# Moving four element-wise steps of a recurrent stage to GpSimd, one square to VectorE, and dropping three matmul uses

## The chip, the cores and the metric

One core of a Trainium2 chip runs the whole program. The metric is device time in microseconds (us) of one execution. TensorE (PE in the rows) does matmuls, VectorE (DVE), ScalarE (ACT) and GpSimd (POOL) do element-wise work, SyncE (SP) issues transfers. Each engine works through its own list of instructions in order and waits on semaphores that other engines raise.

## The reference, cut to what matters

The model has 12 sub-layers; each is followed by a layer norm over the 128 features, so that what enters a stage has mean zero over the features. The changed one is the seventh, a stack of four recurrent layers (RWKV) on 8192 tokens (128 sequences of 64 tokens), 128 features:

```python
for l in range(4):
    h = layer_norm(x, ln1_w[l]); prev = time_shift(h)        # prev: the token before
    k, v = (mix of h and prev by tm_mix_k / tm_mix_v) @ tm_k_w / tm_v_w
    r = sigmoid((h * tm_mix_r + prev * (1 - tm_mix_r)) @ tm_r_w)
    x = x + (r * wkv_scan(k, v, decay, first)) @ tm_o_w
    h = layer_norm(x, ln2_w[l]); prev = time_shift(h)
    kk = (h * cm_mix_k + prev * (1 - cm_mix_k)) @ cm_k_w      # 128 -> 512
    vv = square(relu(kk)) @ cm_v_w                            # 512 -> 128
    rr = sigmoid((h * cm_mix_r + prev * (1 - cm_mix_r)) @ cm_r_w)
    x = x + rr * vv
return layer_norm(x, lnf_w)
```

`wkv_scan` is a recurrence over the tokens: a running maximum, a numerator and a denominator, both weighted by exponentials, and their quotient.

## The kernel before, in words

Function `rwkv` (L2121) is this stage. Features lie on the 128 partitions, tokens along the free side; all is float32. A tile is 512 tokens (8 sequences of 64), so a layer has 16 tiles and the stage 64 *turns* m = 0 to 63 (layer = m // 16). The residual stream `xw` stays in SBUF, centred over the features: matmuls with `center` (identity minus 1/128) keep it so.

A matmul of 512 columns is issued as two instructions on 128x512 float32; I count such a pair as one *call*. A turn has these steps, by engine:

- TensorE: `variance1` (1 call), `keys` (2: now and previous token), `values` (2), `receptance` (1, on an input mixed beforehand), `output` (1), `variance2` (1), `receptance2` (2: `rnow` on the token, `rold` on the token before, summed in PSUM), `hidden` in two halves (4), `contract` in two halves (4), `centred` (1). In the first 16 turns `enter` (L2192, 1 call) makes the centred copy of the input.
- ScalarE: `copy_entered` (first 16 turns), `square1`, `rstd1` (Ln, Exp), `half_mixed_r`, `exp_ab`, `exp_g`, `ln_denominator`, `exp_r`, `ln_r`, `reciprocal`, `square2`, `rstd2`, `half_mixed`, `rectified` and `squared` for each half of the hidden layer (1024 elements a partition each), `exp_rr`, `ln_rr`, `sigmoid_rr`.
- VectorE: `normal1` (L2484) writes hp1, `mix_r`, `running_max`, `exponents_ab` (two instructions), `exponent_g`, `clamp_g`, `clamp_r`, `weighted`, `scan_den`, `scan_num`, `bonus`, `numerator`, `denominator` (L2569), `denominator_r` (L2576), `quotient` (L2581), `residual1` (L2586), `normal2` (L2590) writes hp2, `mix_k`, `clamp_rr`, `gated`, `residual2`. Between turns of the first layer `prepare(l)` scales the weights of layer l.
- GpSimd has nothing to do in this stage. SyncE issues the loads of the weights, seven to a layer, and then the loads of the next stages.

The order on each engine is written out by `interleaved` (L168): each step has a place in us, turn m's copy of it stands at m * PERIOD + place (PERIOD 17.9), and all are sorted by that number. These numbers order the instructions of one engine and nothing else; the semaphores set the time. So about four turns are in flight at once: while TensorE does `variance1` of turn m, it does `keys` of m-1, `output` of m-2 and `hidden` of m-3. After the last layer 16 short end turns (`end_sum`, `end_close` and others) make the final norm; their first ones are interleaved with the last main turns.

```python
    order = sorted((start + (m - first) * period + place, g, j, m) for g, (first, turns, start, period, steps) in enumerate(groups)
                   for j, (place, _) in enumerate(steps) for m in range(first, first + turns))
```

Of the kernel before, what the change touches and what calls it, by code (L numbers as in the profile page):

```python
# [2120 lines left out]
def rwkv(nc, k, d, ahead=()):  # L2121
# [6 lines left out]
    with ExitStack() as ctx:  # L2128
# [62 lines left out]
        def _(pe):
            def enter(m):  # L2192
                if m:
                    pe.wait_ge(ln1, m)
# [99 lines left out]
            interleaved((0, NT, 0, PERIOD, ((0.0, enter),)),  # L2294
                        (0, TURNS, 0, PERIOD, (
                            (10.1, variance1), (20.6, keys), (25.6, values), (24.1, receptance), (44.6, output),
                            (52.6, variance2), (59.8, lambda m: hidden(m, 0)), (58.7, receptance2),
                            (63.5, lambda m: hidden(m, 1)), (70.3, lambda m: contract(m, 0)),
                            (70.8, lambda m: contract(m, 1)), (76.1, centred))),
                        (TURNS, NT, END, END_PERIOD, ((3.2, variance1), (16.2, end_sum), (21.2, end_variance2))))  # L2300

        @block.scalar
        def _(act):
# [125 lines left out]
            interleaved((0, NT, 0, PERIOD, ((4.2, copy_entered),)),  # L2429
                        (0, TURNS, 0, PERIOD, (  # L2430
                            (5.4, square1), (20.8, half_mixed_r), (16.8, rstd1), (28.1, exp_r), (36.8, ln_r),
                            (38.5, ln_denominator), (31.6, exp_ab), (30.3, exp_g), (41.1, reciprocal),
                            (50.5, square2), (53.2, rstd2), (57.8, half_mixed),
                            (62.7, lambda m: rectified(m, 0)), (63.4, lambda m: squared(m, 0)),
                            (67.5, lambda m: rectified(m, 1)), (69.9, lambda m: squared(m, 1)),
                            (61.6, exp_rr), (62.1, ln_rr), (63.9, sigmoid_rr))),
                        (TURNS, NT, END, END_PERIOD, ((0.0, square1), (6.8, rstd1), (17.5, end_square2), (24.4, end_rstd2))))

        @block.vector
        def _(dve):  # L2440
# [128 lines left out]
            def denominator(m):  # L2569
                dve.wait_ge(g_ready, m + 1)  # L2570
                dve.wait_ge(den_ready, m + 1)
                if m:
                    dve.wait_ge(ln_low, m)
                dve.tensor_tensor(flat(dn[:])[:, :, 1:S], ex[:, 0, :, 1:S], den[:, :, 0:S - 1], ALU.add).then_inc(low, 1)

            def denominator_r(m):  # L2576
                dve.wait_ge(ln_low, m + 1)
                dve.wait_ge(er_ready, m + 1)
                dve.tensor_tensor(tokens(dl[:]), er[:], tokens(dl[:]), ALU.add).then_inc(low_r, 1)

            def quotient(m):  # L2581
                dve.wait_ge(rec, m + 1)
                dve.wait_ge(top, m + 1)
                dve.tensor_tensor(gv[:], gv[:], tokens(dl[:]), ALU.mult).then_inc(wkv, 1)

            def residual1(m):  # L2586
                dve.wait_ge(o_mm, m + 1)
                dve.tensor_tensor(xw[:, at(m)[1]], xw[:, at(m)[1]], ps[:, 1, :], ALU.add).then_inc(xc2, 1)

            def normal2(m):  # L2590
                dve.wait_ge(rs2, m + 1)
                if m:
                    dve.wait_ge(rr_mm, m)
                dve.tensor_tensor(hp2[:, :, 1:S1], flat(xw[:, at(m)[1]]), flat(rsb[:]), ALU.mult).then_inc(h2, 1)
# [22 lines left out]
            def end_close(m):  # L2617
# [6 lines left out]
                            (21.3, normal1), (30.4, mix_r), (32.3, clamp_r), (31.0, running_max), (34.3, exponents_ab),  # L2624
                            (31.9, exponent_g), (32.7, clamp_g), (37.0, weighted), (37.7, scan_den), (38.2, scan_num),
                            (34.9, bonus), (40.0, numerator), (39.1, denominator), (42.8, denominator_r),
                            (49.4, quotient), (52.7, residual1), (60.2, normal2), (62.6, mix_k), (66.0, clamp_rr),
                            (75.9, gated), (80.3, residual2))),
                        (1, NL - 1, PERIOD, PERIOD, ((21.3, prepare),)),
                        (TURNS, NT, END, END_PERIOD, ((15.8, normal1), (33.6, end_close))))  # L2630


# [1338 lines left out]
```

## Time and profile before

| | us |
|---|---|
| median of 3 runs (4816.67 to 4822.48) | 4822.15 |
| the profiled execution | 4821.5 |
| its span, first to last instruction | 4819.6 |
| the stage `rwkv` in it, 1859.5 to 3001.8 | 1142.3 |
| TensorE busy in the stage | 1125.4 |
| VectorE busy in the stage | 995.6 |
| ScalarE busy in the stage | 961.9 |
| GpSimd busy in the stage | 0 |

The busy times are unions of the intervals of the instructions; two neighbouring instructions of an engine overlap a little, so that the distance between two starts (called a *slot* below) is shorter than the duration of the first. A row of a timeline has the start in us, the duration in us, engine, line, operation, output and inputs; in brackets the idle time before it and what ended it. "L_attn_ps" and "L_xattn_ps" are PSUM, all other tiles SBUF; "L_attn_er" stands for `er` and `er2`, "L_attn_hp" for `hp1` and `hp2`.

### The profile page before, as it was taken

The numbers are of one execution on the slowest core, as the hardware profiler recorded it, in microseconds if no ns is written. First come the engines' busy times: TensorE is split into PE (matmuls) and PEld (weight loads), VectorE is DVE, ScalarE is ACT, GpSimd is POOL, SyncE is SP. The second block draws the span as 40 slices with busy tenths as digits, with TensorE's granted clock in tenths as the row PEclk, the third lists the DMA queues.
The fourth block names the chain that finished last, engine by engine and source line by source line (L and its number), as shares of the span: only waits on it lengthen the run. The fifth ranks groups of instructions, "written<-read, shape, count | busy, mean of one in ns | idle before, by whom it ended". The sixth has DMA issues, their size and how long they took to land. (4 is left out here: it accounts for less than half of the span.)

```text
span 4819.6 us, 101682 instructions
## 1 busy us (share of the span) xinstructions
PE 4417.6 (92%) x37631; PEld 2907.1 (60%) x37631; DVE 3409.0 (71%) x5379; ACT 3123.7 (65%) x5579; POOL 1471.2 (31%) x1948
## 2 busy tenths in 40 slices
PE   8999788889969987999999999789979989999888
PEld 6767556557757764444444444467657767777665
DVE  7978777567763337889999995653349966666748
ACT  6878677567764336888888888653248844444356
POOL 3444354114407760000000000047734412222327
PEclk9999999889989999999999999899999999999999
DMA  3000000000021122000000000311130000000110
GB/s 106 3 2 3 2 1 1 1 13 3 3 63 51 52 69 84 1 1 1 1 1 1 1 1 20 110 31 53 53 104 3 3 2 1 1 2 1 57 55 36
DMA packets 124460, 119.57 MB, mean 25 GB/s; under 512 B 19536, under 2 KB 104528, under 8 KB 123216
## 3 DMA queue, kind: packets, MB, share of 16 engines
q1 hardware_dynamic: 106576, 77.38, 5.2%
q0 software_dynamic: 17408, 35.69, 2.6%
q8 instruction: 318, 5.21, 0.5%
q14 instruction: 158, 1.29, 0.1%
HBM read 82.60 MB, written 30.41 MB: 23 GB/s over the span
## 5 line engine op out<-in xcount | busy, mean ns | idle before, releaser
L2683 POOL TENSOR_TENSOR L_xattn_E<-L_xattn_E,L_xattn_rz 128x256 f32<-128x256 f32 x16 | 10.2, 635 | 1277.6 <-DVE L_xattn_rz L2839 1277.6
L1759 POOL DMA_INDIRECT L_ffn_xg<-L_ffn_xrows,L_ffn_take x272 | 263.2, 968 | 281.1 <-DVE L_ffn_take L2054 198.8
L1823 PEld LDWEIGHTS L_ffn_ps<-L_ffn_early_down,L_ffn_mT 128*128 128x128 f32 x1904 | 246.8, 191 | 105.8 <-issue 79.8
L1765 POOL DMA_INDIRECT L_ffn_yrows<-L_ffn_yo,L_ffn_put x272 | 268.3, 987 | 99.8 <-issue 59.8
L1803 PE MATMUL L_ffn_ps<-L_ffn_up,L_ffn_xT 128*128 x544 | 259.2, 559 | 19.6 <-issue 8.1
L2919 POOL TENSOR_TENSOR L_xattn_E<-L_xattn_E,L_xattn_rz 128x1024 f32<-128x1024 f32 x64 | 123.7, 1932 | 471.5 <-DVE L_xattn_rz L3139 471.5
L1823 PE MATMUL L_ffn_ps<-L_ffn_early_down,L_ffn_mT 128*128 x1904 | 259.0, 276 | 2.5 <-DVE L_ffn_yo L2084 1.3
L2263 PE MATMUL L_attn_ps<-L_attn_rl,L_attn_wcv 128*128 128x512 f32 x512 | 240.6, 592 | 0.0
L2247 PE MATMUL L_attn_ps<-L_attn_mix,L_attn_wck 128*128 128x512 f32 x512 | 240.6, 592 | 0.0
L1913 ACT ACTIVATE L_ffn_mT<-L_ffn_ps 128x512 f32<-128x512 f32 x136 | 81.2, 597 | 236.9 <-PE L_ffn_ps L1812 236.9
L2073 DVE TENSOR_TENSOR L_ffn_m<-L_ffn_b,L_ffn_ps 128x512 f32<-128x512 f32 x136 | 93.6, 688 | 188.4 <-PE L_ffn_ps L1803 188.4
L2069 DVE TENSOR_TENSOR L_ffn_m<-L_ffn_sg,L_ffn_ps 128x352 f32<-128x352 f32 x136 | 70.9, 521 | 212.3 <-ACT L_ffn_sg L1903 212.3
L988 DVE TENSOR_REDUCE L_xattn_mx<-L_xattn_ps 128x16 f32<-128x1024 f32 x128 | 156.1, 1219 | 69.0 <-PE L_xattn_ps L812 69.0
L334 POOL TENSOR_TENSOR L_attn_Kbd<-L_attn_Kt,main_head_of_row 128x1024 f32<-128x1024 f32 x64 | 121.1, 1893 | 258.0 <-issue 249.5
L750 POOL TENSOR_TENSOR L_xattn_Kbd<-L_xattn_Kt,main_head_of_row 128x1024 f32<-128x1024 f32 x64 | 121.1, 1892 | 238.8 <-issue 233.1
L565 DVE TENSOR_TENSOR L_attn_ps<-L_attn_ps,L_attn_bias 128x512 f32<-128x512 f32 x256 | 164.9, 690 | 20.6 <-PE L_attn_ps L398 20.5
L1095 POOL TENSOR_SCALAR L_ffn_aq<-L_ffn_aq,L_ffn_qinv 128x512 f32<-128x512 f32 x64 | 126.9, 1997 | 165.0 <-ACT L_ffn_aq L1245 165.0
L2263 PEld LDWEIGHTS L_attn_ps<-L_attn_rl,L_attn_wcv 128*128 128x128 f32 x512 | 97.4, 190 | 122.4 <-issue 122.4
L2247 PEld LDWEIGHTS L_attn_ps<-L_attn_mix,L_attn_wck 128*128 128x128 f32 x512 | 92.7, 190 | 127.0 <-issue 92.7
L586 DVE TENSOR_REDUCE L_attn_mx<-L_attn_ps 128x16 f32<-128x1024 f32 x128 | 156.3, 1221 | 3.3
L824 PE MATMUL L_xattn_ps<-main_ident,L_xattn_E 128*128 128x128 f32 x1024 | 145.6, 281 | 14.1 <-ACT L_xattn_Qt L875 10.2
L596 DVE TENSOR_TENSOR L_attn_E<-L_attn_ps,L_attn_mx 128x1024 f32<-128x1024 f32 x128 | 156.1, 1220 | 2.3
(616 smaller groups left out, 13175.0 us busy)
## 6 DMA issues: line engine op xcount, KB each, us to landing
L_ffn_row_hot<-L_ffn_yrows SPq DMA_DIRECT2D x32, 256.0 KB, 3.0
L_ffn_col_hot<-L_ffn_yrows SPq DMA_DIRECT2D x32, 256.0 KB, 3.4
L_ffn_w<-in_L_ffn_e_W SPq DMA_DIRECT2D x32, 256.0 KB, 4.3
L_ffn_xrows<-L_ffn_xtok SPq DMA_DIRECT2D x42, 192.0 KB, 2.1
L_ffn_xg<-L_ffn_xrows,L_ffn_take POOLq DMA_INDIRECT x272, 2.5
L_ffn_yrows<-L_ffn_yo,L_ffn_put POOLq DMA_INDIRECT x272, 2.3
main_x<-in_xT SPq DMA_DIRECT2D x8, 512.0 KB, 7.5
main_ctx<-in_ctxT SPq DMA_DIRECT2D x4, 1024.0 KB, 11.5
```

What stands on the lines that cost most here:

```text
L565: b = dve.tensor_tensor(scores if in_place else E[t % 2][:, 8 * at:8 * at + 8, :].rearrange("p (a h) k -> p a (h k)", a=2), scores, bias_s ...
L586: dve.tensor_reduce(mx[t % 2][:, 16 * half:16 * half + 16], score_rows(half, t), AX, ALU.max) \
L596: dve.tensor_tensor(E[u][:, rows, :], score_rows(half, t), mx[u][:, rows].rearrange("p (a o) -> p a o", o=1).to_broadcast([P, 16, S]), ALU ...
L824: m = pe.transpose(to[:, j * P:(j + 1) * P], E[t % 2][:, row:row + 2, :], k["ident"][:])
L988: dve.tensor_reduce(mx[t % 2][:, 16 * half:16 * half + 16], score_rows(half), AX, ALU.max) \
L1095: m = pool.tensor_scalar(aq[u][:, j, :], aq[u][:, j, :], ROUND, qinv[u][:, 1, j:j + 1], ALU.subtract, ALU.mult)
L1759: pool.indirect_dma_start(xg[t % RING][:], None, xrows, bass.IndirectOffsetOnAxis(ap=take[:, t:t + 1], axis=0)) \
L1765: pool.indirect_dma_start(yrows, bass.IndirectOffsetOnAxis(ap=put[:, t:t + 1], axis=0), yo[t % RING][:], None).then_inc(scattered[t % RING ...
L1803: g = pe.matmul(ps[u][:, 0, 0:F], xT[u][:], up[:, bass.ds(at, F)], start=True, stop=True)
L1823: g = pe.matmul(ps[1][:, 3, 0:P], mT[u][0:rows[a], a * P:(a + 1) * P], down[a][:, bass.ds(at, P)], start=(a == 0), stop=(a == FT - 1))
L2247: r = pe.matmul(ps[:, 5 + a % 2, :], wck[:, at(m)[0], a * P:(a + 1) * P], mix[:], start=True, stop=True)
L2263: r = pe.matmul(ps[:, 7, :], wcv[:, at(m)[0], a, :], rl[:, a, :], start=(a == 0), stop=(a == FT - 1))
```

## The change

Receptance2's input is mixed before the matmul: ScalarE's new `half_mixed_r2` and VectorE's new `mix_r2` make `rmix2`, and `receptance2` is one call on it; `rold`, its load and its scaling go. `denominator`, `denominator_r`, `quotient` and `normal2` go from VectorE's list to a list of GpSimd. The square of the second hidden half goes from ScalarE to VectorE, as a product of the tile with itself. `enter` and `copy_entered` go; the first layer reads `xres` in their place. All places are new; PERIOD and the end turns' period are not.

```diff
-                for tile, j in ((wo, 3), (rnow, 4), (rold, 4)):
+                for tile, j in ((wo, 3), (rnow, 4)):
...
-            def enter(m):
-                if m:
-                    pe.wait_ge(ln1, m)
-                pe.matmul(ps[:, 0, :], center[:], xres[:, m * CT:(m + 1) * CT], start=True, stop=True).then_inc(c_mm, 1)
...
             def receptance2(m):
-                pe.wait_ge(h2, m + 1)
+                pe.wait_ge(rmixed2, m + 1)
                 if m:
                     pe.wait_ge(z, m)
-                pe.matmul(ps[:, 7, :], rnow[:, l, :], hp2[:, :, 1:S1], start=True, stop=False)
-                pe.matmul(ps[:, 7, :], rold[:, l, :], hp2[:, :, 0:S], start=False, stop=True).then_inc(rr_mm, 1)
+                pe.matmul(ps[:, 7, :], rnow[:, l, :], rmix2[:], start=True, stop=True).then_inc(rr_mm, 1)
...
+            interleaved((0, TURNS, 0, PERIOD, (
+                            (6.8, variance1), (20.0, keys), (27.3, values), (32.9, receptance), (46.1, output),
+                            (52.9, variance2), (61.4, lambda m: hidden(m, 0)), (61.0, receptance2),
+                            (66.5, lambda m: hidden(m, 1)), (71.2, lambda m: contract(m, 0)),
+                            (72.1, lambda m: contract(m, 1)), (76.8, centred))),
...
-                act.activation(sqa[:], xw[:, at(m)[1]], ACT.Square).then_inc(sq1, 1)
+                act.activation(sqa[:], before(m), ACT.Square).then_inc(sq1, 1)
...
+            def half_mixed_r2(m):
+                l = at(m)[0]
+                act.wait_ge(h2, m + 1)
+                if m:
+                    act.wait_ge(rr_mm, m)
+                act.activation(flat(rmix2[:]), hp2[:, :, 1:S1], ACT.Identity, scale=cnow[:, l, 1:2]).then_inc(half_rmix2, 1)
...
+            interleaved((0, TURNS, 0, PERIOD, (
+                            (-9.1, square1), (13.3, half_mixed_r), (-0.9, rstd1), (28.8, exp_r), (30.9, ln_r),
+                            (28.3, ln_denominator), (19.4, exp_ab), (23.8, exp_g), (34.0, reciprocal),
+                            (38.7, square2), (45.3, rstd2), (48.7, half_mixed), (48.0, half_mixed_r2), (54.9, lambda m: rectified(m, 0)), (55.1, squared),
+                            (60.1, lambda m: rectified(m, 1)),
+                            (61.0, exp_rr), (64.2, ln_rr), (64.5, sigmoid_rr))),
...
+        @block.gpsimd
+        def _(pool):
+            def denominator(m):
+                pool.wait_ge(g_ready, m + 1)
+                pool.wait_ge(den_ready, m + 1)
+                if m:
+                    pool.wait_ge(ln_low, m)
+                pool.tensor_tensor(flat(dn[:])[:, :, 1:S], ex[:, 0, :, 1:S], den[:, :, 0:S - 1], ALU.add).then_inc(low, 1)
+
+            def denominator_r(m):
+                pool.wait_ge(ln_low, m + 1)
+                pool.wait_ge(er_ready, m + 1)
+                pool.tensor_tensor(tokens(dl[:]), er[:], tokens(dl[:]), ALU.add).then_inc(low_r, 1)
+
+            def quotient(m):
+                pool.wait_ge(rec, m + 1)
+                pool.wait_ge(top, m + 1)
+                pool.tensor_tensor(gv[:], gv[:], tokens(dl[:]), ALU.mult).then_inc(wkv, 1)
+
+            def normal2(m):
+                pool.wait_ge(rs2, m + 1)
+                if m:
+                    pool.wait_ge(mixed, m)
+                    pool.wait_ge(rmixed2, m)
+                pool.tensor_tensor(hp2[:, :, 1:S1], flat(xw[:, at(m)[1]]), flat(rsb[:]), ALU.mult).then_inc(h2, 1)
+
+            pool.wait_ge(w_steps, 1)
+            staggered(TURNS, PERIOD, (39.9, denominator), (48.8, denominator_r), (50.0, quotient), (58.1, normal2))
...
+            def mix_r2(m):
+                l = at(m)[0]
+                dve.wait_ge(half_rmix2, m + 1)
+                dve.scalar_tensor_tensor(flat(rmix2[:]), hp2[:, :, 0:S], cold[:, l, 1:2], flat(rmix2[:]), ALU.mult, ALU.add) \
+                    .then_inc(rmixed2, 1)
+
+            def squared(m):
+                dve.wait_ge(relu, 2 * m + 2)
+                dve.tensor_tensor(rl[:, 2:4, :], rl[:, 2:4, :], rl[:, 2:4, :], ALU.mult).then_inc(srb, 1)
...
+            interleaved((0, TURNS, 0, PERIOD, (
+                            (14.8, normal1), (22.4, mix_r), (32.4, clamp_r), (25.1, running_max), (25.5, exponents_ab),
+                            (25.7, exponent_g), (27.3, clamp_g), (32.5, weighted), (30.7, scan_den), (35.1, scan_num),
+                            (36.7, bonus), (40.6, numerator), (44.9, residual1), (55.1, mix_k), (54.7, mix_r2), (68.0, squared),
+                            (61.4, clamp_rr),
+                            (72.4, gated), (74.0, residual2))),
```

Sorted by these places, one stretch of the changed lists reads:

- VectorE: gated, bonus, mix_r2, mix_k, residual2, mix_r, numerator, running_max, exponents_ab (2), clamp_rr, exponent_g, residual1, clamp_g, scan_den, squared, clamp_r, weighted, normal1, scan_num.
- ScalarE: rectified (first half), squared (first half), exp_ab, square2, exp_g, rectified (second half), exp_rr, square1, rstd2 (2), ln_denominator, ln_rr, sigmoid_rr, exp_r, half_mixed_r2, half_mixed, ln_r, half_mixed_r, reciprocal, rstd1 (2).
- GpSimd: denominator, normal2, denominator_r, quotient.
- TensorE: contract (second half), keys, centred, variance1, receptance2, hidden (first), values, output, hidden (second), receptance, variance2, contract (first).

## Rows read from the trace of the kernel before

**Rows 1.** Busy times by window: us, then busy us (instructions) per engine, PEclk, DMA

```profile
2200.00:2400.00 200.00, 200.00 (x467) 86.80 (x466) 184.46 (x271) 171.97 (x260) 0.00 (x0) 1.00 0.00 1
...
1859.50:3001.80 1142.30, 1125.42 (x2592) 483.84 (x2592) 995.63 (x1486) 961.94 (x1458) 0.00 (x0) 0.99 0.02 5
```

**Rows 2.** Timeline of TensorE in the first layer and in a later one

```profile
2052.04 1.02 PE L2195 MATMUL L_attn_ps<-main_x,main_center 128*128 128x512 f32 x2
...
2069.21 1.02 PE L2195 MATMUL L_attn_ps<-main_x,main_center 128*128 128x512 f32 x2
...
2514.68 1.02 PE L2255 MATMUL L_attn_ps<-L_attn_hp,L_attn_rnow 128*128 128x512 f32 x2
2515.54 1.02 PE L2256 MATMUL L_attn_ps<-L_attn_hp,L_attn_rold 128*128 128x512 f32 x2
...
2530.99 1.02 PE L2255 MATMUL L_attn_ps<-L_attn_hp,L_attn_rnow 128*128 128x512 f32 x2
```

**Rows 3.** Timeline of VectorE in a later layer of the stage

```profile
2504.53 0.41 DVE L2534 TENSOR_SCALAR L_attn_ex<-L_attn_ex 128x504 f32<-128x504 f32 x1
2504.85 0.74 DVE L2520 SCALAR_TENSOR_TENSOR L_attn_ex<-L_attn_mm,L_attn_rate 128x504 f32<-128x504 f32 x1
2505.51 0.68 DVE L2521 TENSOR_TENSOR L_attn_ex<-L_attn_ps,L_attn_mm 128x504 f32<-128x504 f32 x1
2506.10 0.68 DVE L2588 TENSOR_TENSOR L_attn_xw<-L_attn_xw,L_attn_ps 128x512 f32<-128x512 f32 x1
...
2507.89 1.22 DVE L2547 TENSOR_TENSOR_SCAN L_attn_den<-L_attn_ex 128x512 f32<-128x512 f32 x1
2509.03 1.20 DVE L2554 TENSOR_TENSOR_SCAN L_attn_num<-L_attn_ex,L_attn_bv 128x512 f32<-128x512 f32 x1
```

**Rows 4.** GpSimd's groups over the whole span: busy us, mean ns of one

```profile
L3254 POOL TENSOR_TENSOR L_gather_half<-L_gather_D 128x512 f32<-128x512 f32 x16 | 20.3, 1272 | 5.1 <-DVE L_gather_D L3397 5.1
```

**Rows 5.** Timeline of VectorE and GpSimd in the last stage

```profile
4749.33 2.49 POOL L3570 TENSOR_TENSOR L_combine_Kbd<-L_combine_K,L_combine_early_diag 128x1024 f32<-128x1024 f32 x1
...
4750.92 1.45 DVE L3777 TENSOR_TENSOR main_x<-main_x,L_combine_rs 128x512 f32<-128x512 f32 x1
4751.79 2.37 POOL L3586 TENSOR_TENSOR L_combine_E<-L_combine_E,L_combine_rz 128x1024 f32<-128x1024 f32 x1
4752.30 1.21 DVE L3744 TENSOR_REDUCE L_combine_mx<-L_combine_ps 128x64 f32<-128x1024 f32 x1
4753.43 0.73 DVE L3772 SCALAR_TENSOR_TENSOR main_x<-L_combine_ps,L_combine_bo,main_x 128x512 f32<-128x512 f32 x1
```

**Rows 6.** Timeline of VectorE and GpSimd in the stage after

```profile
3077.82 0.68 DVE L2849 TENSOR_TENSOR main_x<-main_x,L_xattn_rs 128x512 f32<-128x512 f32 x1
3077.98 0.99 POOL L2683 TENSOR_TENSOR L_xattn_E<-L_xattn_E,L_xattn_rz 128x256 f32<-128x256 f32 x1 [3.25 <-DVE L_xattn_rz L2839]
```

**Rows 7.** Same GpSimd line, all 16 instructions: ns min/median/max, first and last start

```profile
L2683 POOL TENSOR_TENSOR L_xattn_E<-L_xattn_E,L_xattn_rz x16: 607/612/986, 3007.9 to 3078.0; 128x256 f32<-128x256 f32 x16
```

**Rows 8.** Timeline of VectorE, the longest instruction of L3777

```profile
4712.18 10.32 DVE L3777 TENSOR_TENSOR main_x<-main_x,L_combine_rs 128x512 f32<-128x512 f32 x1
```

**Rows 9.** Timeline of ScalarE in a later layer of the stage

```profile
2507.16 1.01 ACT L2390 ACTIVATE L_attn_rl<-L_attn_ps 128x1024 f32<-128x1024 f32 x1
2508.08 0.62 ACT L2369 ACTIVATE L_attn_sqb<-L_attn_xw 128x512 f32<-128x512 f32 x1
...
2510.79 0.67 ACT L2375 ACTIVATE L_attn_rsb<-L_attn_ps,main_misc 128x512 f32<-128x512 f32 x1
2511.49 0.63 ACT L2377 ACTIVATE L_attn_rsb<-L_attn_rsb 128x512 f32<-128x512 f32 x1
2512.03 0.61 ACT L2344 ACTIVATE L_attn_er<-L_attn_er 128x512 f32<-128x512 f32 x1
...
2513.07 0.71 ACT L2336 ACTIVATE L_attn_rmix<-L_attn_hp,L_attn_tnow 128x512 f32<-128x512 f32 x1
2513.70 0.72 ACT L2384 ACTIVATE L_attn_mix<-L_attn_hp,L_attn_cnow 128x512 f32<-128x512 f32 x1
```

More of the change, by code:

```diff
@@ L2142, in rwkv @@
         ex, bv = s.sb("ex", [P, 3, NB, S]), s.sb("bv", [P, NB, S])
-        gv, dn, er, er2, mix, rmix = (s.sb(x, [P, CT]) for x in ("gv", "dn", "er", "er2", "mix", "rmix"))
+        gv, dn, er, er2, mix, rmix, rmix2 = (s.sb(x, [P, CT]) for x in ("gv", "dn", "er", "er2", "mix", "rmix", "rmix2"))
         rl = s.sb("rl", [P, FT, CT])
         ps = s.psum("ps")[0]
-        col_loaded, w_steps, rate_exp, ready, c_mm, entered = (s.sem(x) for x in (
-            "col_loaded", "w_steps", "rate_exp", "ready", "c_mm", "entered"))
+        col_loaded, w_steps, rate_exp, ready = (s.sem(x) for x in ("col_loaded", "w_steps", "rate_exp", "ready"))
         w_loaded = [s.sem(f"w_loaded{l}") for l in range(NL)]
@@ L2167, in at, with before @@
             return l, slice(n * CT, (n + 1) * CT)
+        def before(m):
+            l, tokens_of = at(m)
+            return (xres if l == 0 else xw)[:, tokens_of]
         def flat(t):
@@ L2292, in end_variance2 @@
                 pe.matmul(ps[:, 4, :], avg[:], rmix[:], start=True, stop=True).then_inc(evar2, 1)
[L2294 to L2300, printed above, removed]
+            interleaved((0, TURNS, 0, PERIOD, (
[3 more added lines that the diff above has]
+                            (72.1, lambda m: contract(m, 1)), (76.8, centred))),
+                        (TURNS, NT, END, END_PERIOD, ((6.3, variance1), (18.9, end_sum), (22.1, end_variance2))))
         @block.scalar
@@ L2306, in _ @@
             act.activation(rate[:], col[:, :, 4], ACT.Exp).then_inc(rate_exp, 1)
-            def copy_entered(m):
-                act.wait_ge(c_mm, m + 1)
-                act.activation(xw[:, m * CT:(m + 1) * CT], ps[:, 0, :], ACT.Copy).then_inc(entered, 1)
             def square1(m):
-                if m < NT:
-                    act.wait_ge(entered, m + 1)
-                else:
+                if m >= NT:
                     act.wait_ge(xc3, m - NT + 1)
@@ L2390, in rectified @@
                 act.activation(rl[:, 2 * half:2 * half + 2, :], ps[:, 5:7, :], ACT.Relu).then_inc(relu, 1)
-            def squared(m, half):
-                act.wait_ge(relu, 2 * m + 1 + half)
-                act.activation(rl[:, 2 * half:2 * half + 2, :], rl[:, 2 * half:2 * half + 2, :], ACT.Square).then_inc(sr, 1)
+            def squared(m):
+                act.wait_ge(relu, 2 * m + 1)
+                act.activation(rl[:, 0:2, :], rl[:, 0:2, :], ACT.Square).then_inc(sra, 1)
             def exp_rr(m):
@@ L2427, in end_rstd2 @@
                 act.activation(tokens(mm[:]), tokens(mm[:]), ACT.Exp, scale=-0.5).then_inc(ers2, 1)
[L2429 to L2437, printed above, removed]
+            interleaved((0, TURNS, 0, PERIOD, (
[4 more added lines that the diff above has]
+                            (61.0, exp_rr), (64.2, ln_rr), (64.5, sigmoid_rr))),
+                        (TURNS, NT, END, END_PERIOD, ((-5.2, square1), (1.7, rstd1), (12.7, end_square2), (17.8, end_rstd2))))
@@ L2491, in normal1 @@
                     dve.wait_ge(rmixed, m)
-                dve.tensor_tensor(hp1[:, :, 1:S1], flat(xw[:, at(m)[1]]), flat(rsa[:]), ALU.mult).then_inc(h1, 1)
+                dve.tensor_tensor(hp1[:, :, 1:S1], flat(before(m)), flat(rsa[:]), ALU.mult).then_inc(h1, 1)
             def mix_r(m):
@@ L2567, in numerator @@
                 dve.tensor_tensor(flat(gv[:])[:, :, 1:S], flat(gv[:])[:, :, 1:S], num[:, :, 0:S - 1], ALU.add).then_inc(top, 1)
[L2569 to L2584, printed above, removed]
             def residual1(m):
                 dve.wait_ge(o_mm, m + 1)
[L2588 to L2594, printed above, removed]
+                dve.tensor_tensor(xw[:, at(m)[1]], before(m), ps[:, 1, :], ALU.add).then_inc(xc2, 1)
             def mix_k(m):
@@ L2623, in _ @@
             interleaved((0, TURNS, 0, PERIOD, (
[L2624 to L2630, printed above, removed]
+                            (14.8, normal1), (22.4, mix_r), (32.4, clamp_r), (25.1, running_max), (25.5, exponents_ab),
[3 more added lines that the diff above has]
+                            (72.4, gated), (74.0, residual2))),
+                        (1, NL - 1, PERIOD, PERIOD, ((-2.6, prepare),)),
+                        (TURNS, NT, END, END_PERIOD, ((10.3, normal1), (27.2, end_close))))
 def padded_attention(nc, k, d, col, early, ahead):
```

17 lines of the change are left out of this document (8 added, 9 removed).

## The prediction

> **What bounds the kernel now.** Read the busy times by window first: in the middle of the stage TensorE is busy 200.00 of 200 us, VectorE 184.46, ScalarE 171.97, GpSimd nothing [rows 1]. Then TensorE's timeline: a matmul call follows the one before it at 0.86 us, and one turn the next at 2530.99 - 2514.68 = 16.31 us, which is 19 calls of 0.858; in the first layer, with `enter`, 2069.21 - 2052.04 = 17.17 us, 20 calls [rows 2]. So TensorE sets the pace, without a gap, and a call that goes is worth 0.86 us in each turn until the next engine is full. That is VectorE, whose queue has 15.54/12.26 = 1.27 us to spare in a turn (idle 15.54 us in a window of 200/16.31 = 12.26 turns) [rows 1].
>
> **What the edits do, engine by engine.** *TensorE:* `receptance2` loses one call in 64 turns, `enter` one in 16. 18 calls give 15.45 us a turn, and if nothing else were late the stage would gain 64 x 0.86 + 16 x 0.86 = 69 us. *VectorE:* slots (start to start) are 0.60 for a tensor_tensor or a clamp from PSUM, 0.66 for a scalar_tensor_tensor, 0.32 for `clamp_g`, 1.14 for a scan [rows 3]. Four of 0.60 go; `mix_r2` adds 0.66 and the square of 1024 elements 1.13 (the slot of the 1024-element instruction in [rows 5], 4753.43 - 4752.30). The new list is 10 x 0.60 + 5 x 0.66 + 3 x 1.13 + 1.13 + 0.32 = 14.1 us, 0.6 less than before and under 15.45. *ScalarE:* a square of 1024 elements goes (a slot of about 0.92, as the one before it has), `half_mixed_r2` adds 0.63 [rows 9]; no bound there. *GpSimd:* four float32 tensor_tensors of 512 with two full inputs, 1.27 us each [rows 4], 5.1 us of 15.45. By busy time all fits under TensorE. *Loads:* one of seven per layer goes (SyncE then comes to the next stages' loads earlier) with one small scaling in `prepare`; I take it at nothing, since the loads of later layers lie under 16 turns each (bounds 0 and -1 us, at the first keys). Without `enter` and `copy_entered` the first turn starts about 1.5 us earlier (a call of 0.86 and a copy like the 0.62 us square of [rows 9]); the other copies lay in ScalarE's idle share.
>
> **What busy times hide.** VectorE and GpSimd don't run freely side by side. In the last stage a VectorE product of two SBUF tiles, usually 0.69 us, starts at 4750.92 and takes 1.45: it ends 0.55 after GpSimd's instruction does (4751.82), so it stood until then and worked afterwards; and the GpSimd instruction that follows takes 2.37 us, because now it waits for VectorE. A VectorE reduction and a scalar_tensor_tensor that read PSUM run beside it in their usual 1.21 and 0.73 [rows 5]. The other way round, a GpSimd instruction issued while VectorE multiplies two SBUF tiles takes 0.99 instead of 0.61: VectorE's end, 3078.50, plus 0.47 [rows 6, 7]. So one with two SBUF inputs and one on GpSimd exclude each other for a whole instruction, and the first comer wins. These rows show it for tensor_tensor alone. The Trainium skill (SBUF — State Buffer, section "SBUF: two separate sides") names every VectorE instruction with two SBUF inputs, against a GpSimd instruction that reads SBUF, and every one in a two-port mode; by it mixes and scans collide too, as in my likeliest case, and without it the sum is that of rival 1.
>
> In the new list 7.5 us of VectorE's 14.1 read two SBUF tiles (all mixes, `numerator`, the first of `exponents_ab`, `scan_den`, `scan_num`, `squared`, `normal1`; `clamp_g` may count too). I follow one turn from the moment VectorE's slot of `residual1` ends (0), with a hand-over between engines of 0.07. A blocked 512-element product frees VectorE 0.48 after GpSimd's end (4752.30 - 4751.82 [rows 5]); I take 0.54 for a scalar_tensor_tensor and 1.0 for 1024 elements.
>
> 1. `clamp_g` 0.32, `scan_den` done at 1.54; GpSimd's `denominator` 1.61 to 2.88. `squared` cannot be there first: ScalarE does square2 (from 0.12), exp_g, rectified (0.52, 0.52, 1.01 [rows 9]) and releases it at 2.2. VectorE is free again at 3.88 instead of 2.59 (0.32 + 2 x 1.13).
> 2. `clamp_r`, `weighted`: 5.08. ScalarE meanwhile: exp_rr, square1, Ln, Exp of rstd2 (slot 0.92 of rectified, 0.52, 0.52, 0.70, duration 0.63) end at 4.45, so GpSimd's `normal2` holds 4.52 to 5.79 and `normal1` ends its slot at 6.27 instead of 5.68. `scan_num`, `gated`, `bonus`: 8.60.
> 3. ScalarE: after Exp (slot 0.54) ln_denominator 0.52, ln_rr 0.67 (its follower depends on it), sigmoid 0.52, exp_r 0.52, two mixes 0.63 each, ln_r 0.61: 8.46. GpSimd's `denominator_r` holds 8.53 to 9.80, just ahead of `mix_r2` (8.60), which frees VectorE at 10.34 instead of 9.26. Behind it in VectorE's list stand `mix_k` and `residual2`, and TensorE's `receptance2` and `hidden` wait for all three.
> 4. `mix_k`, `residual2`, `mix_r`: 12.26. `numerator` has its result at 12.94, `quotient` 13.01 to 14.28; `running_max` reads PSUM and isn't blocked, but the first of `exponents_ab` is, to 14.82. The second, `clamp_rr`, `exponent_g`, `residual1` (0.60 + 0.60 + 0.66 + 0.60): 17.28.
>
> That is the turn: 17.28 us, 14.1 of work and 3.2 lost to four waits. TensorE then stands 1.8 us a turn, at `centred` (for `gated`), `receptance2` and `hidden`. Break-even is 16.50 (below).
>
> **The sum.** Of 64 turns about 60 run at the steady pace, 13 of them of the first layer (its other three pass in the fill): before 13 x 17.17 + 47 x 16.31 = 989.8 us, 16.50 on average; after 60 x 17.28 = 1036.8. Fill and drain: four GpSimd steps 0.6 us longer each and one more mix of 0.63 + 0.66 in the first turn's chain, against the entry's 1.5 us: +2, estimated, within -4 to +6. The end turns keep their instructions: 0. Against the profiled execution (4821.5, 0.65 under the median shown): 4821.5 + 47 + 2 = 4870.5; I forecast 4870.
>
> **Rivals.**
> 1. *Only plain tensor_tensors collide* (what the rows show at the least). `mix_r2` and `exponents_ab` pass; waits 1 and 2 stay (both products): 14.1 + 1.3 + 0.6 = 16.0 us a turn, 960 against 989.8, -30 + 2: 4793. Faster; this is the other side, and the point that decides is whether a turn stays under 16.50, so whether wait 3 (1.08) exists. For it: no row has a mix beside GpSimd. Against: it reads two SBUF tiles in the same way.
> 2. *VectorE wins at `mix_r2`* and keeps its place through `mix_k`: 8.60 against 8.53 is closer than I can work it out. Then `denominator_r` runs 9.9 to 11.15, `mix_r` is what waits, and the turn is 16.66: 60 x 0.16 + 2 = +12: 4833. If GpSimd gets in between the two mixes, it is 17.27 again.
> 3. *The waits don't matter*, as GpSimd's work falls in the 6.6 us of VectorE's PSUM instructions: TensorE stays the bound, 15.45 a turn, 927 + 2: -61, 4761. For it: 5.1 is less than 6.6. Against: three of the four come free exactly where VectorE turns to SBUF.
> 4. *GpSimd keeps others out longer*: one VectorE product stood 10.3 us behind four GpSimd instructions in a row [rows 8]. If each blocked step costs 0.25 more (18.3 us a turn): +108, 4930.
>
> **Chances.** Forecast 0.50; rivals 0.15, 0.15, 0.12, 0.08. A measurement of this kernel can tell about 0.2% (9.6 us) from no change. Rival 2 sits at that edge and is split in two. Slower: 0.50 + 0.08 + half of 0.15 = 0.65, cut to 0.62 since the forecast rests on small margins; same 0.10; faster 0.28. The range takes in rivals 1 and 2 and the lower part of 4, leaving out rival 3: 4785 to 4900. The likeliest case's own range, with a turn of 17.0 to 17.6 and the fill's bounds, is 4848 to 4894.
>
> **What would show it.** Right: GpSimd instructions of 1.3 us, some longer; VectorE's `squared`, `normal1` and `mix_r2` with durations of 1.3 to 2 us, while `gated`, `weighted`, `clamp_r`, `running_max` keep theirs; `receptance2` starts 17.3 us apart; TensorE busy near 90% there, waiting for VectorE in gaps of under 1 us, with its granted clock still at 1.00 (the level of 2.4 GHz). Step 3 is wrong if `mix_r2` takes 0.74; rival 3 is right if TensorE is again busy 200 of 200 and the starts lie 15.45 apart. The whole is wrong if VectorE products beside GpSimd keep 0.69 us.

## The result and the profile after

The changed kernel takes 4859.04 us (median of 4 runs, 4856.68 to 4860.47) against 4819.41 for the kernel before beside it (4 runs, 4816.11 to 4822.48): ratio 1.0082, 95% interval [1.0064, 1.0099], so 39.6 us slower. Forecast: 4870. The profiled execution took 4860.47, its span is 4858.6.

The time went into the pace of the turns. One step in each turn marks it: all 64 instructions of `mix_k` and the last closing product of the stage, the kernel before first (number, ns min/median/max, first and last start).

```profile
L2599 DVE SCALAR_TENSOR_TENSOR L_attn_mix<-L_attn_hp,L_attn_cold,L_attn_mix x64: 744/744/752, 1901.3 to 2946.4; 128x512 f32<-128x512 f32 x64
...
L2621 DVE TENSOR_TENSOR main_x<-L_attn_ps,L_attn_mm x16: 680/684/692, 2929.9 to 3001.1; 128x512 f32<-128x512 f32 x16
```

The same two lines of the changed kernel:

```profile
L2598 DVE SCALAR_TENSOR_TENSOR L_attn_mix<-L_attn_hp,L_attn_cold,L_attn_mix x64: 737/739/1754, 1899.2 to 2983.6; 128x512 f32<-128x512 f32 x64
...
L2630 DVE TENSOR_TENSOR main_x<-L_attn_ps,L_attn_mm x16: 675/684/693, 2969.7 to 3039.9; 128x512 f32<-128x512 f32 x16
```

The first turn comes 2.1 us earlier, the 63 distances between first and last take 1084.4 instead of 1045.1 (+39.3), the way from the last one to the stage's last closing product 56.3 instead of 54.7 (+1.6); behind the stage the two spans differ by 0.2. Sum +39.0, the difference of the spans.

Busy times in the middle of the stage, as in [rows 1]: TensorE no longer has all of the window (189.24 of 200 us), VectorE has more than before (192.25 against 184.46) although its list is shorter.

```profile
2200.00:2400.00 200.00, 189.24 (x418) 74.26 (x417) 192.25 (x232) 159.44 (x247) 59.22 (x47) 1.00 0.00 1
```

TensorE's timeline, the calls beside which it stands and the next turn's first; the starts of `receptance2` (L2253) lie 17.18 us apart, where [rows 2] had 16.31:

```profile
2500.89 1.12 PE L2253 MATMUL L_attn_ps<-L_attn_rmix,L_attn_rnow 128*128 128x512 f32 x2 [0.32 <-DVE L_attn_rmix L2604]
2502.24 1.95 PE L2245 MATMUL L_attn_ps<-L_attn_mix,L_attn_wck 128*128 128x512 f32 x4 [0.23 <-DVE L_attn_xw L2624]
...
2514.05 1.12 PE L2202 MATMUL L_attn_ps<-L_attn_hp,L_attn_now 128*128 128x512 f32 x2 [0.34 <-DVE L_attn_hp L2514]
...
2518.07 1.13 PE L2253 MATMUL L_attn_ps<-L_attn_rmix,L_attn_rnow 128*128 128x512 f32 x2 [0.32 <-DVE L_attn_rmix L2604]
```

VectorE's timeline through one turn, `clamp_g` to `clamp_g`, some steps left out:

```profile
2507.65 0.41 DVE L2556 TENSOR_SCALAR L_attn_ex<-L_attn_ex 128x504 f32<-128x504 f32 x1
...
2509.85 1.82 DVE L2609 TENSOR_TENSOR L_attn_rl<-L_attn_rl 128x1024 f32<-128x1024 f32 x1 [0.66 <-ACT L_attn_rl L2387]
2511.59 0.68 DVE L2526 TENSOR_SCALAR L_attn_er<-L_attn_ps 128x512 f32<-128x512 f32 x1
2512.19 0.67 DVE L2563 TENSOR_TENSOR L_attn_bv<-L_attn_ex,L_attn_ps 128x512 f32<-128x512 f32 x1
2512.78 1.21 DVE L2514 TENSOR_TENSOR L_attn_hp<-L_attn_xw,L_attn_rsa 128x512 f32<-128x512 f32 x1
2513.92 1.21 DVE L2576 TENSOR_TENSOR_SCAN L_attn_num<-L_attn_ex,L_attn_bv 128x512 f32<-128x512 f32 x1
...
2516.23 1.79 DVE L2604 SCALAR_TENSOR_TENSOR L_attn_rmix<-L_attn_hp,L_attn_cold,L_attn_rmix 128x512 f32<-128x512 f32 x1
2517.94 0.74 DVE L2598 SCALAR_TENSOR_TENSOR L_attn_mix<-L_attn_hp,L_attn_cold,L_attn_mix 128x512 f32<-128x512 f32 x1
...
2520.46 1.21 DVE L2533 TENSOR_TENSOR_SCAN L_attn_mm<-L_attn_decay,L_attn_ps 128x512 f32<-128x512 f32 x1
2521.70 0.79 DVE L2542 SCALAR_TENSOR_TENSOR L_attn_ex<-L_attn_mm,L_attn_rate 128x504 f32<-128x504 f32 x1
2522.41 0.67 DVE L2543 TENSOR_TENSOR L_attn_ex<-L_attn_ps,L_attn_mm 128x504 f32<-128x504 f32 x1
...
2524.84 0.41 DVE L2556 TENSOR_SCALAR L_attn_ex<-L_attn_ex 128x504 f32<-128x504 f32 x1
```

GpSimd's in the same stretch (`denominator`, `normal2`, `denominator_r`, `quotient`):

```profile
2509.33 1.26 POOL L2441 TENSOR_TENSOR L_attn_dn<-L_attn_ex,L_attn_den 128x504 f32<-128x504 f32 x1 [4.57 <-ACT L_attn_ex L2343]
2512.17 1.28 POOL L2458 TENSOR_TENSOR L_attn_hp<-L_attn_xw,L_attn_rsb 128x512 f32<-128x512 f32 x1 [1.59 <-ACT L_attn_rsb L2367]
2516.20 1.27 POOL L2446 TENSOR_TENSOR L_attn_dl<-L_attn_er,L_attn_dl 128x512 f32<-128x512 f32 x1 [2.76 <-ACT L_attn_er L2334]
2520.68 1.27 POOL L2451 TENSOR_TENSOR L_attn_gv<-L_attn_gv,L_attn_dl 128x512 f32<-128x512 f32 x1 [3.21 <-DVE L_attn_gv L2589]
```

All instructions of `normal1`'s line in the kernel before:

```profile
L2492 DVE TENSOR_TENSOR L_attn_hp<-L_attn_xw,L_attn_rsa x80: 681/692/694, 1869.5 to 2994.5; 128x512 f32<-128x512 f32 x80
```

Lay them beside each other. `normal1`, 0.68 to 0.69 us before, takes 1.21 because `normal2` came 0.61 ahead of it; `mix_r2` takes 1.79 because `denominator_r` came 0.03 us ahead of it, and ends 0.55 behind it; `squared` (L2609) takes 1.82, where e1 and e3 below have 1.22 and 1.23, because `denominator` came 0.52 ahead of it. `weighted` (L2563) and `running_max` (L2533), which read PSUM, lie beside `normal2` and `quotient` and keep 0.67 and 1.21. For these waits no idle time is shown: they stand in the duration. The 0.66 us of idle time ahead of `squared` is another wait, for the `rectified` of ScalarE (L2387).

### The profile page after: what moved, and what is told of

The parts are those of the page before. It is cut to its first block and busy times, and to the rows that moved or that the text cites. A ratio compares the mean times of both kernels' runs of the same rounds, so it can differ in the third digit from the quotient of the medians.

```text
span 4858.6 us, 101510 instructions
## 1 busy us (share of the span) xinstructions
PE 4402.8 (91%) x37471; PEld 2864.6 (59%) x37471; DVE 3499.1 (72%) x5243; ACT 3097.4 (64%) x5563; POOL 1796.3 (37%) x2204
## 5 line engine op out<-in xcount | busy, mean ns | idle before, releaser
L2441 POOL TENSOR_TENSOR L_attn_dn<-L_attn_ex,L_attn_den 128x504 f32<-128x504 f32 x64 | 80.6, 1259 | 375.1 <-ACT L_attn_ex L2343 288.1
L2387 ACT ACTIVATE L_attn_rl<-L_attn_ps 128x1024 f32<-128x1024 f32 x128 | 129.8, 1014 | 128.1 <-PE L_attn_ps L2245 128.1
L1095 POOL TENSOR_SCALAR L_ffn_aq<-L_ffn_aq,L_ffn_qinv 128x512 f32<-128x512 f32 x64 | 126.8, 1996 | 168.3 <-ACT L_ffn_aq L1245 168.3
L2202 PE MATMUL L_attn_ps<-L_attn_hp,L_attn_now 128*128 128x512 f32 x256 | 140.6, 631 | 29.7 <-DVE L_attn_hp L2514 29.7
```

The source lines that it names most:

```text
L1095: m = pool.tensor_scalar(aq[u][:, j, :], aq[u][:, j, :], ROUND, qinv[u][:, 1, j:j + 1], ALU.subtract, ALU.mult)
L2202: pe.matmul(ps[:, bank, :], now[:, 3 * l + j, :], hp1[:, :, 1:S1], start=True, stop=False)
L2387: act.activation(rl[:, 2 * half:2 * half + 2, :], ps[:, 5:7, :], ACT.Relu).then_inc(relu, 1)
```

## Experiments

**The place of one step.** e1 edits VectorE's list of the changed kernel:

```diff
-(68.0, squared),
+(68.4, squared),
```

> The changed kernel with one place altered: VectorE's square of the second hidden half stands after clamp_r and weighted instead of before them, so that GpSimd's first sum runs beside two VectorE instructions that read PSUM. Theory (VectorE instructions with two SBUF inputs and GpSimd's shut each other out): VectorE is past these three steps at 3.88 us after residual1 instead of 5.08, normal1 goes ahead of GpSimd's normal2, and the turn falls from 17.19 us to about 15.65: near 4767 us (up to 4830 if GpSimd gets in between normal1 and scan_num). Rival (the loss is GpSimd's longer latency, 1.27 us against 0.66, along the chain of the turn, with no exclusion): the square comes 1.2 us later for contract, so the turn stays at 17.2 us or grows: 4859 us or more.

Measured: 4823.48 (4820.11 to 4826.55) against 4817.8, ratio 1.001 [1.0001, 1.002]; `receptance2` 16.63 us apart. One place of 19 gives back some 35 us, and the second branch of the expectation is what came: `squared` and `mix_r2` are short (1.22 and 0.74), but GpSimd now gets in ahead of `scan_num`, as that branch says, and ahead of `mix_k`, which it doesn't name. VectorE, e1:

```profile
2404.99 0.69 DVE L2514 TENSOR_TENSOR L_attn_hp<-L_attn_xw,L_attn_rsa 128x512 f32<-128x512 f32 x1
2405.59 2.30 DVE L2576 TENSOR_TENSOR_SCAN L_attn_num<-L_attn_ex,L_attn_bv 128x512 f32<-128x512 f32 x1
...
2409.65 1.75 DVE L2598 SCALAR_TENSOR_TENSOR L_attn_mix<-L_attn_hp,L_attn_cold,L_attn_mix 128x512 f32<-128x512 f32 x1
```

GpSimd, e1: `normal2` is issued while `normal1` runs and is 0.08 longer for it.

```profile
2405.45 1.35 POOL L2458 TENSOR_TENSOR L_attn_hp<-L_attn_xw,L_attn_rsb 128x512 f32<-128x512 f32 x1 [1.58 <-ACT L_attn_rsb L2367]
```

**The close race.** e2 moves `bonus` behind `mix_k`, so that `mix_r2` starts 0.6 us sooner. "The port" is the expectations' word for what GpSimd and a VectorE instruction with two SBUF inputs cannot have at once.

```diff
-(36.7, bonus),
+(37.7, bonus),
```

> The changed kernel with one place altered: VectorE's bonus stands after mix_k instead of before mix_r2, so that mix_r2 can start 0.6 us earlier, about 0.5 us ahead of GpSimd's denominator_r. Theory, if VectorE keeps the port through mix_r2 and mix_k: denominator_r waits for both and then runs beside bonus and residual2, which read PSUM; the turn falls to about 16.2 us: near 4800 us. Theory, if GpSimd gets the port between the two mixes: mix_k is held instead of mix_r2 and the turn stays at 17.2 us: 4859 us. Rival (latency alone): bonus is on no chain that GpSimd lengthens: 4859 us.

Measured: 4855.72 (4853.07 to 4856.67), ratio 1.0072 [1.0055, 1.0089], 17.15 us a turn. VectorE wins at `mix_r2` and loses at the next instruction: `denominator_r` (2412.35) was issued while `mix_r2` ran. VectorE and GpSimd, e2:

```profile
2411.78 0.74 DVE L2604 SCALAR_TENSOR_TENSOR L_attn_rmix<-L_attn_hp,L_attn_cold,L_attn_rmix 128x512 f32<-128x512 f32 x1
2412.45 1.75 DVE L2598 SCALAR_TENSOR_TENSOR L_attn_mix<-L_attn_hp,L_attn_cold,L_attn_mix 128x512 f32<-128x512 f32 x1
...
2412.35 1.29 POOL L2446 TENSOR_TENSOR L_attn_dl<-L_attn_er,L_attn_dl 128x512 f32<-128x512 f32 x1 [2.75 <-ACT L_attn_er L2334]
```

**The exclusion taken away.** e3 keeps order, waits and GpSimd's durations (1.24 us) and takes away its reads; the results of the four steps are left out. One of the four:

```diff
-pool.tensor_tensor(tokens(dl[:]), er[:], tokens(dl[:]), ALU.add).then_inc(low_r, 1)
+pool.memset(idle[0][:], 0.0).then_inc(low_r, 1)
```

> The changed kernel, with GpSimd's four steps put in place by fills of a scratch tile of 128 x 1366 float32 (about 1.27 us by the fill of 128 x 1024 in 0.95 us), with all waits and signals kept; the sums, the products and hp2 are not computed and the clamp of the exponent is 0. GpSimd then reads no SBUF. Theory (the port is taken by what reads): VectorE's instructions keep their short durations, TensorE is the bound again at 15.45 us a turn: near 4755 us. Rival (latency alone): the four steps last as long as before, so the turn stays at 17.2 us: 4859 us. If fills shut VectorE out as well, the theory's part on reading falls and the time stays at 4859 us with stretched VectorE instructions.

Measured: 4747.12 (4745.54 to 4753.13), ratio 0.9847 [0.9831, 0.9864]. TensorE has all of the window again:

```profile
2200.00:2400.00 200.00, 200.00 (x468) 88.56 (x467) 187.18 (x260) 177.24 (x273) 64.33 (x52) 1.00 0.00 1
```

GpSimd meets VectorE at the same places as before, here `normal2`'s fill 0.03 us ahead of `normal1`, which keeps its short duration:

```profile
2401.00 1.24 POOL L2459 MEMSET L_attn_idle<- 128x1366 f32 x1 [1.61 <-ACT L_attn_rsb L2368]
...
2401.03 0.69 DVE L2516 TENSOR_TENSOR L_attn_hp<-L_attn_xw,L_attn_rsa 128x512 f32<-128x512 f32 x1
```

So 112 us of the changed kernel's time (1.74 us a turn, 17.19 to 15.45) go with GpSimd's reads, that is with the exclusion; that a step takes twice as long on GpSimd as on VectorE costs nothing that shows.

**No GpSimd at all.** e4 is the kernel before with the mix ahead of `receptance2` and without `enter`; half of its edit:

```diff
-pe.matmul(ps[:, 7, :], rnow[:, l, :], hp2[:, :, 1:S1], start=True, stop=False)
-pe.matmul(ps[:, 7, :], rold[:, l, :], hp2[:, :, 0:S], start=False, stop=True).then_inc(rr_mm, 1)
+pe.matmul(ps[:, 7, :], rnow[:, l, :], rmix2[:], start=True, stop=True).then_inc(rr_mm, 1)
...
-(62.6, mix_k),
+(62.5, mix_r2), (62.6, mix_k),
```

> The kernel before with two parts of the change alone: receptance2's input mixed beforehand (half_mixed_r2 and mix_r2 just ahead of their counterparts), and the entry's centring dropped. The four steps stay on VectorE, both squares on ScalarE, the other places are those of before. TensorE needs 15.45 us a turn; VectorE's slots are 14.75 + 0.66 = 15.4 us. Theory: nothing is shut out, VectorE and TensorE are about equally full, a turn takes 15.5 to 16.2 us: 4755 to 4800 us. Rival (mixing beforehand, with its longer chain to receptance2, is what costs): 17.2 us a turn, 4859 us.

Measured: 4859.04 (4858.42 to 4863.81), ratio 1.0084 [1.0067, 1.0101], 17.16 us a turn: a miss, and the time that the rival gave. I had summed work and not followed a ring. The number of the changed kernel comes out for another reason, which TensorE's timeline shows: `centred` (L2265), then nothing until `receptance2` (L2253).

```profile
2430.92 1.02 PE L2265 MATMUL L_attn_ps<-L_attn_er,main_center 128*128 128x512 f32 x2
2433.39 1.13 PE L2253 MATMUL L_attn_ps<-L_attn_rmix,L_attn_rnow 128*128 128x512 f32 x2 [1.44 <-DVE L_attn_rmix L2600]
```

VectorE's list of before has `residual2` (L2616) there, which waits for `centred`; `mix_r2` (L2600) stands behind it although its input was ready:

```profile
2431.98 0.69 DVE L2616 TENSOR_TENSOR L_attn_xw<-L_attn_xw,L_attn_ps 128x512 f32<-128x512 f32 x1 [0.61 <-PE L_attn_ps L2265]
2432.59 0.74 DVE L2600 SCALAR_TENSOR_TENSOR L_attn_rmix<-L_attn_hp,L_attn_cold,L_attn_rmix 128x512 f32<-128x512 f32 x1
```

In before the two calls of `receptance2` needed only hp2 and covered that time [rows 2]. e7 tests it with one place of e4:

```diff
-(62.5, mix_r2),
+(61.55, mix_r2),
```

> The kernel of e4_no_gpsimd with one place moved: `mix_r2` 62.5 to 61.55, so that VectorE does it ahead of `residual2`. Theory from the trace of e4: TensorE stands 1.4 us a turn because `receptance2`, now in need of `mix_r2`, is behind the ring `centred`, `residual2`, `mix_r2`; with the swap `mix_r2` runs while `centred` does. Turn 16.5 us, time 4820 (4810 to 4830). Rival, that the mix's own chain (`normal2`, half on ScalarE, `mix_r2`) is too long whatever the order: 17.16 us, 4859.

Measured: 4825.21 (4816.42 to 4830.47) against 4821.76, ratio 1.001 [1.0001, 1.002], 16.54 us a turn: the ring was worth 0.62 us of 17.16. The rest is the mix's own chain, which the rival named: of the 1.09 us a turn that e7 still takes over 15.45, 0.58 lies ahead of `receptance2`, which waits for `mix_r2`, which in turn waits for its half from ScalarE; some 0.5 lies at `hidden`, which starts when `mix_k` behind them ends. TensorE and VectorE, e7:

```profile
2416.09 1.12 PE L2253 MATMUL L_attn_ps<-L_attn_rmix,L_attn_rnow 128*128 128x512 f32 x2 [0.42 <-DVE L_attn_rmix L2600]
...
2415.29 0.75 DVE L2600 SCALAR_TENSOR_TENSOR L_attn_rmix<-L_attn_hp,L_attn_cold,L_attn_rmix 128x512 f32<-128x512 f32 x1 [0.19 <-ACT L_attn_rmix L2381]
```

The changed kernel has `mix_r2` ahead of `residual2` and doesn't pay the ring. Nor is the mix's chain what makes its 17.19: e3 above and e5 below have the same mix and run at 15.45 and 15.56.

**A version that beats both.** e5 moves two places of the changed kernel, found by following the queues as in the prediction, now with the durations of these traces; e6 moves `bonus` alone.

```diff
-(14.8, normal1),
+(14.4, normal1),
...
-(36.7, bonus),
+(31.45, bonus),
```

> The changed kernel with two VectorE places moved and nothing else: `bonus` from 36.7 to 31.45 (between `scan_den` and `squared`) and `normal1` from 14.8 to 14.4 (between `squared` and `clamp_r`). Exclusion theory, with each engine's queue followed with the durations of the traces: GpSimd's `normal2` then arrives 0.05 us behind `normal1` and beside `clamp_r` and `weighted`, which read PSUM; `denominator_r` arrives during `mix_k` and stands 0.3 us itself; only `squared` still stands (0.5 us) and `mix_r` (0.4 us), and VectorE's list is 14.1 + 0.9 us, under TensorE's 15.45. Turn 15.45 us (15.65 if `normal2` gets ahead of `normal1`), time 4755, at most 4775. Rival, that the turn is long because of the longer GpSimd instructions and not because of where they fall: 4859, as the four GpSimd instructions are the same.

> The changed kernel with one place moved: `bonus` 36.7 to 31.45. Exclusion theory: `bonus` fills part of the gap ahead of `squared` and no longer stands between `gated` and `mix_r2`, so `mix_r2` (0.74 us) is on its way when `denominator_r` arrives; GpSimd gets the port between `mix_r2` and `mix_k`, and `mix_k` takes 1.75. `normal1` still takes about 1.2. Turn 16.55 us, time 4820 (4810 to 4830). Rival, that places within VectorE's list make no difference as long as its work is the same: 4859.

Measured: e5 4762.78 (4760.86 to 4765.36) against 4821.76, ratio 0.9884 [0.9868, 0.9899], 15.56 us a turn; e6 4821.45, ratio 1.0003 [0.9993, 1.0012], 16.55 us. In e5 `normal1` has 0.1 us left when `normal2` is issued and is not held up; `denominator_r` comes while `mix_k` runs, and both mixes stay short; VectorE:

```profile
2420.18 0.68 DVE L2514 TENSOR_TENSOR L_attn_hp<-L_attn_xw,L_attn_rsa 128x512 f32<-128x512 f32 x1
...
2423.81 0.75 DVE L2604 SCALAR_TENSOR_TENSOR L_attn_rmix<-L_attn_hp,L_attn_cold,L_attn_rmix 128x512 f32<-128x512 f32 x1
2424.47 0.75 DVE L2598 SCALAR_TENSOR_TENSOR L_attn_mix<-L_attn_hp,L_attn_cold,L_attn_mix 128x512 f32<-128x512 f32 x1
...
2425.74 1.17 DVE L2519 SCALAR_TENSOR_TENSOR L_attn_rmix<-L_attn_hp,L_attn_told,L_attn_rmix 128x512 f32<-128x512 f32 x1
```

GpSimd, e5: the wait is now its own (1.56), and it costs VectorE 0.4 at `mix_r`.

```profile
2420.76 1.28 POOL L2458 TENSOR_TENSOR L_attn_hp<-L_attn_xw,L_attn_rsb 128x512 f32<-128x512 f32 x1 [1.58 <-ACT L_attn_rsb L2367]
2424.79 1.56 POOL L2446 TENSOR_TENSOR L_attn_dl<-L_attn_er,L_attn_dl 128x512 f32<-128x512 f32 x1 [2.76 <-ACT L_attn_er L2334]
```

**Parts alone.** e8, the entry dropped from the kernel before:

```diff
-interleaved((0, NT, 0, PERIOD, ((0.0, enter),)),
-            (0, TURNS, 0, PERIOD, (
+interleaved((0, TURNS, 0, PERIOD, (
```

> The kernel before with one part of the change alone: the centring matmul at entry and the copy behind it are dropped, and the first layer reads the residual stream where it lies. Theory: a turn of the first layer goes from 17.17 to 16.31 us, 12 of them by the trace of before (10.3 us), and the first turn starts 1.5 us earlier: 4806 (4804 to 4809). Rival, that the entry's matmul was hidden: 4818.

Measured: 4810.42 (4804.79 to 4815.94), just above the expected range; 11.3 under the 4821.76 beside it, where 12 were expected, while the ratio of 0.9985 [0.9976, 0.9994] comes to some 7 us. In the profiled executions the last closing product of the stage starts at 2990.2 instead of 3001.1, 10.9 earlier. So the entry is worth 7 to 11 us.

e9 takes `denominator_r` back to VectorE in the changed kernel (first edit), e10 the square to ScalarE (second):

```diff
-staggered(TURNS, PERIOD, (39.9, denominator), (48.8, denominator_r), (50.0, quotient), (58.1, normal2))
+staggered(TURNS, PERIOD, (39.9, denominator), (50.0, quotient), (58.1, normal2))
...
+(36.85, denominator_r),
...
-(68.0, squared),
...
-(55.1, squared), (60.1, lambda m: rectified(m, 1)),
+(55.1, lambda m: squared(m, 0)), (60.1, lambda m: rectified(m, 1)), (60.3, lambda m: squared(m, 1)),
```

> The changed kernel with one of the four GpSimd steps undone: `denominator_r` is on VectorE again, between `mix_r2` and `mix_k`; the other three stay on GpSimd. Exclusion theory: VectorE's work grows by a slot of 0.60 us, but the wait at `mix_r2` (1.05 us a turn) is gone, so the kernel with more VectorE work is the faster one: turn 17.19 - 0.45 = 16.74 us, time 4832 (4825 to 4842), `mix_r2` 0.74 us. Rival, that VectorE's list of work is what sets the turn: 17.19 + 0.60 = 17.79 us, 4895.

> The changed kernel with its square undone: ScalarE squares both halves as before, VectorE has no `squared`; all else as changed. Theory: the 1.74 us slot of `squared` behind `denominator` and the 0.66 us VectorE stands ahead of it go, ScalarE has 0.96 us more, which makes `rstd2` and with it `normal2` later, so that `scan_num` is through ahead of it; VectorE's list of 13.0 us is no longer the bound, but its `gated` waits some 2.8 us for the sigmoid on ScalarE. Turn 16.4 us, time 4811 (4803 to 4822). Rival, that the square on VectorE is what keeps ScalarE from being the bound: 17.19 + 0.96 us, 4910.

Measured against 4818.25: e9 4827.42 (4823.86 to 4833.36), ratio 1.002 [1.0011, 1.0029], 16.74 us a turn; e10 4816.03 (4811.52 to 4818.89), ratio 0.9996 [0.9987, 1.0005], 16.46 us. e9 gives VectorE more work and is some 31 us faster than the changed kernel (4859.04 less 4827.42, from two sittings). VectorE, e9: `mix_r2`, `denominator_r`, `mix_k` in a row without a wait.

```profile
2398.90 0.74 DVE L2604 SCALAR_TENSOR_TENSOR L_attn_rmix<-L_attn_hp,L_attn_cold,L_attn_rmix 128x512 f32<-128x512 f32 x1
2399.56 0.68 DVE L2589 TENSOR_TENSOR L_attn_dl<-L_attn_er,L_attn_dl 128x512 f32<-128x512 f32 x1
2400.16 0.74 DVE L2598 SCALAR_TENSOR_TENSOR L_attn_mix<-L_attn_hp,L_attn_cold,L_attn_mix 128x512 f32<-128x512 f32 x1
```

In e10 `gated` waits for the sigmoid on ScalarE:

```profile
2405.63 0.69 DVE L2617 TENSOR_TENSOR L_attn_er<-L_attn_er,L_attn_ps 128x512 f32<-128x512 f32 x1 [2.63 <-ACT L_attn_er L2404]
```

## Why the prediction was right

- **The bound.** TensorE's 18 calls would be 15.45 us; e3 runs at that, so the calls that went are worth what was said, once nothing else is late. The entry alone gave 7 to 11 us (e8).
- **The mechanism.** Exclusion, not latency and not work: e3 and e9. The first comer wins, as in [rows 5 to 7]; after shows it for a scalar_tensor_tensor (1.79), e1 for a scan with two SBUF inputs (2.30), and instructions that read PSUM pass (`weighted` 0.67, `running_max` 1.21). The Trainium skill (SBUF — State Buffer, section "SBUF: two separate sides") counts every VectorE instruction with two SBUF inputs, and only against a GpSimd instruction that reads SBUF; these rows agree, and so do e3's fills, beside which nothing stands. Rival 1 is out: `mix_r2` does stand.
- **The chain, point by point**, from `residual1`'s slot end (2507.65): behind `squared` 3.88 said, 3.94 measured (2511.59); behind `normal1` 6.27 and 6.27; behind `mix_r2` 10.34 and 10.29; behind the first of `exponents_ab` 14.82 and 14.76; the turn 17.28 and 17.19. The "3.2 lost to four waits" are not all exclusion: 0.66 is VectorE's idle time for `rectified`, ahead of `squared`. By the slots, exclusion holds `squared` up by 0.61, `normal1` by 0.54, `mix_r2` by 1.05 and `exponents_ab` by 0.05, 2.25 us a turn; without it TensorE's 15.45 is the bound, so that 1.74 of them are lost time.
- **The close race.** Said 0.07 us between `denominator_r` and `mix_r2`, measured 0.03. That GpSimd came first, as said, was luck: the hand-over that was put at 0.07 takes 0.04 us from `rectified` to `squared` and 0.14 from `ln_r` to `denominator_r` (ScalarE's L2334 ends at 2516.06). Who wins it hardly matters: in e2 VectorE does, and the turn is 17.15, the branch of rival 2 that was put at 17.27. Where both mixes go first, in e5, `mix_r` is what stands, as that rival said; there `denominator_r` comes only when `mix_k` already runs. Worked out by its own terms, rival 2's other turn is some 16.7 us and not 16.66, and the 7.5 us of work on two SBUF tiles have `clamp_g`'s 0.32 in them; neither moves the forecast.
- **TensorE's stand.** Said 1.8 us at `centred`, `receptance2` and `hidden`; it is 17.19 - 15.45 = 1.74, but at `keys` (for `normal1`) where I had put `centred`, two calls on in its list. TensorE is busy 95% of the window, not near 90%.
- **The size.** +39.0 instead of +49. The turn is 0.09 shorter than said, over 60 turns 5.4 us; the 63 distances took +39.3 where 47 - 5.4 = 41.6 would follow. Fill and drain, put at +2, were -2.1 + 1.6 + 0.2 = -0.3: the first turn's longer chain costs less than the entry gave back. The other 2.3 us lie at the two ends of the stage: the first distance is 1.1 shorter than before (16.59 against 17.69), the next 59 are together 43.6 longer (four of them, one in each layer, take 17.48), and the last three, among the end turns, are 3.2 shorter (52.6 against 55.8). Why the ends are shorter was not followed.
- **Rivals 3 and 4** are refuted, the one by the pace, the other by blocked instructions that cost what the hand sum had. Whether `clamp_g` (one SBUF input) is held up too stays open: no GpSimd instruction lies beside it in any of these runs, and elsewhere in the kernel before the rows go both ways (last section).

## What to carry to other kernels

Work moved to GpSimd is priced by what VectorE does at the moment it arrives: lay VectorE instructions with PSUM operands beside it, and look at the durations, since such a wait shows as a long instruction and not as idle time. Two places in a list of 19 were worth 96 us here (4859 to 4763), more than twice what the change cost. When a matmul's input gets a step of its own, look whether that step is queued behind something that waits for the same engine (e4, e7).

## What the runs showed of the hardware that I had not expected

A waiting GpSimd instruction gets in between two VectorE instructions that follow each other at a slot of 0.66 us (e2: 0.74, then 1.75). A GpSimd fill of 1366 elements, 1.24 us long, holds up no VectorE instruction (e3, with a fill beside each: `normal1` 0.68 to 0.69, `mix_k` and `mix_r` 0.75, `squared` 1.23, `scan_num` 1.22). The first of `exponents_ab` hid most of its wait: it was due 2521.67, when `running_max` ended, GpSimd was through 0.28 later, and it took 0.79 instead of 0.74.

One SBUF input may not always pass. In the kernel before, 14 reductions of an SBUF tile (L3759) beside a GpSimd instruction keep 1.22 us. Of 12 small tensor_scalars (L1288, 128x4) beside one, seven keep 0.17 to 0.19 and five take 0.57 to 0.58, ending within 0.03 us of GpSimd's instruction. One of them starts at 714.06 and ends at 714.64, GpSimd's (L1095) at 714.61. What sets the five apart was not followed.
